# Routing one part of the tokens two slots earlier, and attention's row statistics on ScalarE

## The reference

```python
h = layernorm(patches_of_five_shifted_images @ W.T + b) * gamma + beta      # 36 tokens
h = concatenate([h, vocab[x_txt]], axis=1)                                  # 68 tokens
x = _layernorm(h)
q, k, v = heads(x @ qkv_w.T + qkv_b)                    # 12 heads of 16
_, idx = top_k(_ex_quant(q) @ _ex_quant(k).T, 32)       # exponents only choose the 32 keys
h = h + softmax(true_scores at idx) @ v @ proj_w.T + proj_b
x = _layernorm(h)
w_fk, w_rk = top-4 of softmax((x @ W_fk + b_fk) @ emb_fk_n.T), the same for rk   # of 128 experts each
y = sum over 4 of w_fk * (x @ f_know[e])                # [192] -> [128]
out = h + sum over 4 of w_rk * (y @ r_know[e])          # [128] -> [192]
```

## Time and profile before

| | us |
|---|---|
| median of the runs of before | 963.44 |
| lowest of them | 958.73 |
| the profiled execution, whole | 963.31 |
| its span, first to last instruction | 961.6 |
| mean granted clock of TensorE | 0.841 |
| slots 1 to 32 begin (first and last `sc` addition) | 59.14 to 466.29 |
| first indirect transfer of `send` | 492.86 |
| first product over sorted rows | 550.10 |

### The profile page before, as it was taken

How to read it: one execution, slowest core, us unless ns; L and a number is a source line. 1 busy time by engine, 2 the same in 40 slices (tenths; PEclk the granted TensorE clock), 3 DMA queues, 4 the chain that set the end, 5 groups by cost and what they waited for, 6 DMA issues and landing times.

```text
span 961.6 us, 22280 instructions
## 1 busy us (share of the span) xinstructions
PE 792.3 (82%) x6347; PEld 658.8 (69%) x6347; DVE 657.4 (68%) x4126; ACT 365.6 (38%) x1147; POOL 565.5 (59%) x788
## 2 busy tenths in 40 slices
PE   5789999999999988898664399999998799499800
PEld 4679888888888767776453277999976558355800
DVE  2298999999999979888577367766763364155433
ACT  0133444444444434544323023444431257345700
POOL 5256666767677656575347507506776577775075
PEclk9787989899999868987655579999996899789955
DMA  9332453535353334531047388756799698489533
GB/s 327 107 121 85 182 181 114 183 113 184 114 183 134 114 116 131 173 113 44 13 134 212 121 254 270 221 156 184 243 403 408 224 327 296 147 299 355 194 100 91
DMA packets 81696, 177.25 MB, mean 184 GB/s; under 512 B 12968, under 2 KB 38344, under 8 KB 78760
## 3 DMA queue, kind: packets, MB, share of 16 engines
q1 hardware_dynamic: 56200, 120.62, 37.7%
q10 hardware_dynamic: 14112, 32.12, 8.9%
q0 software_dynamic: 11264, 23.09, 8.0%
HBM read 94.25 MB, written 81.53 MB: 183 GB/s over the span
## 4 chain that ended last, share of the span: by engine, by line
PE 31%; POOL 27%; DVE 16%; issue 14%; DMA 7%; ACT 4%; SPq 1%; POOLq 0%; ACTq 0%; DVEq 0%
POOL early L781 7%; DVE work L1438 6%; PE bank L1301 5%; POOL slots_g L788 5%; DVE top L1432 4%; PE bank L1289 4%; PE bank L1306 3%; POOL slots_x L758 3%; POOL eqbd L653 3%; PE bank L1103 3%; PE bank L1055 2%; PE bank L1035 2%; PE bank L1353 2%; DMA early<-slots_x 2%; POOL sc L704 2%
## 5 line engine op out<-in xcount | busy, mean ns | idle before, releaser
L1438 DVE MATCH_REPLACE8 work<-top,work 128x68 f32<-128x68 f32 x896 | 179.6, 213 | 0.3 <-issue 0.2
L1432 DVE MAX8 top<-work 128x8 f32<-128x68 f32 x896 | 129.3, 215 | 19.7 <-ACT tru L831 19.2
L1740 DVE COPY place<-bank 96x256 f32<-96x256 f32 x147 | 57.1, 416 | 77.2 <-PE bank L1289 73.8
L781 POOL DMA_INDIRECT early<-slots_h,s_all x68 | 65.8, 967 | 57.0 <-DMA slots_h<-m_y 36.9
L758 POOL DMA_INDIRECT slots_x<-early,s_all x68 | 67.8, 998 | 51.1 <-DVE s_all L1622 30.8
L1035 PE MATMUL bank<-early,xp 128*128 128x192 f32 x432 | 92.8, 378 | 5.6 <-DMA xp<-in_a_x 5.2
L781 POOL DMA_INDIRECT early<-slots_y,s_all x68 | 65.2, 959 | 52.2 <-DMA slots_y<-m_y 29.1
L1035 PEld LDWEIGHTS bank<-early,xp 128*128 128x128 f32 x432 | 89.7, 231 | 8.1 <-DMA xp<-in_a_x 5.5
L1748 DVE COPY place<-bank 128x128 f32<-128x128 f32 x147 | 37.6, 287 | 82.3 <-PE bank L1343 80.3
L704 POOL TENSOR_TENSOR sc<-work,tru 128x476 f32<-128x476 f32 x32 | 38.0, 1188 | 78.5 <-ACT work L883 78.5
L788 POOL DMA_INDIRECT slots_g<-early,s_all x68 | 66.4, 976 | 29.9 <-issue 20.1
(11 more groups left out here) (202 smaller groups left out, 1861.7 us busy)
## 6 DMA issues: line engine op xcount, KB each, us to landing
early<-slots_x SPq DMA_DIRECT2D x49, 384.0 KB, 4.1
slots_y<-m_y ACTq DMA_DIRECT2D x49, 384.0 KB
slots_h<-m_y ACTq DMA_DIRECT2D x49, 256.0 KB
early<-slots_g SPq DMA_DIRECT2D x49, 256.0 KB
f_all<-in_f_know SPq DMA_DIRECT2D x16, 768.0 KB, 8.8
r_all<-in_r_know SPq DMA_DIRECT2D x16, 768.0 KB
slots_x<-zero SPq DMA_DIRECT2D x28, 360.0 KB, 3.0
slots_x<-zero SPq DMA_DIRECT2D x28, 336.0 KB, 3.3
```

The source lines that it names most:

```text
L781: nc.gpsimd.indirect_dma_start(g_in[:, i % DEPTH, k, 0:width], None, src, bass.IndirectOffsetOnAxis(s_all[:, r - 1, i, k:k + 1], 0)).then_ ...
L1432: last = nc.vector.max(top8[:, c, :], work[:, par, c, :])
L1438: last = nc.vector.match_replace(work[:, par, c, :], top8[:, c, :], work[:, par, c, :], TAKEN)
L1740: nc.vector.tensor_copy(m_xT[t][0:HALF], turn_bank[t][0:HALF, 0:2 * P].rearrange("p (c s) -> p c s", c=2)).then_inc(sem["m_xt0"], 1)
```

## The change

Part one is routed in slots 22 to 30 (`ROUTE0` is 22). The embedding runs at 8 products a slot throughout and so ends in slot 20, and its last norm is in slot 21. The counting of part one, which stood between slots 32 and 33, is done inside slot 31, and `find_slots` of the first tile inside slot 32. `ahead_of` goes on after part one: tiles 9, 10 and 11 are normalised in slots 30, 31 and 32. GpSimd's slot 33 is gone; its two `finish` steps stand between the first sends.

`norm` leaves VectorE. ScalarE forms the mean by a Copy and the sum of squares by a Square, each with an accumulated output, at the place in the slot where `scale` stood, and `scale` moves behind `copy_scores`. In a routing slot TensorE's `t_query` moves ahead of `attend`, and `t_logits` ahead of `keep_busy` and `t_position`.

The tables and the issuing engine SP:

```diff
-ROUTE0 = 24
+ROUTE0 = 22
...
-    EMBED_AT.setdefault(_n // 8 if _n < 48 else 6 + max(_n - 49, 0) // 7, []).append((2 + _n // CHUNKS_K, _n % CHUNKS_K))
+    EMBED_AT.setdefault(_n // 8, []).append((2 + _n // CHUNKS_K, _n % CHUNKS_K))
...
-            return routed(b + 1)
+            return b + 1 - ROUTE0 if ROUTE0 <= b + 1 <= BATCH + 1 else None
+        NEXT = BATCH + 2 - ROUTE0
...
-                if b in (20, 30, BATCH + 1):
+                if b in (19, 27, 31, BATCH + 1):
...
-                if b == 20:
+                if b == 19:
```

GpSimd:

```diff
-                nc.gpsimd.tensor_tensor(mv[:, 4:5], mv[:, 0:1], minus_one[0:n, :], ALU.mult)
-                nc.gpsimd.tensor_tensor(mv[:, 2:3], mv[:, 1:2], eps_col[0:n, :], ALU.add).then_inc(sem["ln_eps"], 1)
+                nc.gpsimd.tensor_scalar(mv[:, 2:3], mv[:, 1:2], 1.0 / D, EPS, ALU.mult, ALU.add).then_inc(sem["ln_eps"], 1)
...
-                if b == BATCH + 1:
-                    finish(b - 2, par)
...
+            pool.wait_ge(sem["slots_zeroed"], 4 * 16 * N_ZERO)
+            send(0)
+            finish(BATCH - 2, 0)
+            send(1)
+            finish(BATCH - 1, 1)
+            for i in range(NEXT - 4, NT):
...
-            slot(BATCH + 1, 1)
-            pool.wait_ge(sem["slots_zeroed"], 4 * 16 * N_ZERO)
-            for i in range(LED - 1, NT):
-                t_step(i)
-                send(i - LED + 1)
-            for i in range(NT - LED + 1, NT):
+                send(i - NEXT + 6)
```

ScalarE:

```diff
+            def norm(b, par):
+                act.wait_ge(sem[f"hb_in{par}"], own16(b, par))
+                if runs(b, 1, BATCH):
+                    act.wait_ge(sem["ln_done"], b)
+                nc.scalar.activation(xn_flat[:], hb[:, par, :], ACT.Copy, scale=-1.0 / D, accum_out=mv[:, 0:1]).then_inc(sem["ln_stat"], 1)
+                act.wait_ge(sem["ln_stat"], b + 1)
+                nc.scalar.activation(xn_flat[:], hb[:, par, :], ACT.Square, bias=mv[:, 0:1], accum_out=mv[:, 1:2]).then_inc(sem["ln_aggr"], 1)
...
-                    scale(b + 2, par)
+                    norm(b + 2, par)
...
+                if runs(b, 0, BATCH - 3):
+                    scale(b + 2, par)
```

TensorE:

```diff
+                if b == ROUTE0 + LED:
+                    count_part(0)
...
+                if i is not None:
+                    t_query(i)
...
-                if i is not None:
-                    t_query(i)
+                if b == ROUTE0 + LED:
+                    turn_counts(0)
...
-                    if b < BATCH:
-                        keep_busy(i)
+                    t_logits(i)
+                    keep_busy(i)
...
-                    t_logits(i)
...
+                if b == ROUTE0 + LED:
+                    sum_counts(0)
...
-            t_position(LED - 1)
-            count_part(0)
-            turn_counts(0)
-            for i in range(LED - 4, LED - 1):
-                t_step(i)
-            sum_counts(0)
+            t_step(LED - 2)
```

VectorE:

```diff
-            def norm(b, par):
-                dve.wait_ge(sem[f"hb_in{par}"], own16(b, par))
-                nc.vector.bn_stats(stat[:, 0:6], hb[:, par, :]).then_inc(sem["ln_stat"], 1)
-                dve.wait_ge(sem["ln_stat"], b + 1)
-                plain()
-                nc.vector.bn_aggr(mv[:, 0:2], stat[:, 0:6]).then_inc(sem["ln_aggr"], 1)
...
+                counting = b == ROUTE0 + LED
+                if b == BATCH:
+                    find_slots(0, 0)
...
+                if counting:
+                    take_counts(0)
...
-                if runs(b, 0, BATCH - 3):
-                    norm(b + 2, par)
...
+                if counting:
+                    form_counts(0)
...
+                if counting:
+                    form_base(0)
+                    clear_of(0)
...
-            take_counts(0)
-            form_counts(0)
-            form_base(0)
-            clear_of(0)
+            for i in range(1, 4):
+                find_slots(0, i)
```

More of the change, by code:

```diff
@@ L842, in _ @@
             act.wait_ge(sem["biases_in"], 16 * 8)
+            norm(0, 0)
             scale(0, 0)
@@ L846, in _ @@
             copy_scores(0, 0)
+            norm(1, 1)
             scale(1, 1)
@@ L962, in _ @@
             slots_of(act, slot)
-            t_placed(LED - 1)
-            for i in range(LED - 4, LED - 1):
-                t_step(i)
+            t_step(LED - 2)
             slot(BATCH + 1, 1)
@@ L1483, in _ @@
             nc.vector.tensor_tensor(row_b[:, 0, :], bank[1][:, 0:D], row_b[:, 0, :], ALU.add).then_inc(sem["row_ready"], 1)
-            norm(0, 0)
             quantise(0, 0)
-            norm(1, 1)
             def slot(b, m):
@@ L1504, in slot @@
                 i = routed(b)
-                if i is not None and not take:
-                    t_rank(i)
+                if counting:
+                    take_counts(0)
                 if take:
@@ L1528, in slot @@
                     t_aggregate(ahead_of(b))
+                if counting:
+                    form_counts(0)
                 if take:
                     take8(b, par, 2)
-                if i is not None and take:
+                if i is not None:
                     t_rank(i)
+                if counting:
+                    form_base(0)
+                    clear_of(0)
                 if embeds:
@@ L1683, in t_step @@
             def t_step(i):
-                if follows(i + 4):
+                if NEXT <= i + 4 < NT:
                     t_stats(i + 4)
```

31 lines of the change are left out of this document (17 added, 14 removed).

## The result

| | before | after |
|---|---|---|
| median of the runs, us | 961.47 | 1003.46 |
| the profiled execution, whole | 963.31 | 1003.92 |
| its span | 961.6 | 1001.7 |
| mean granted clock | 0.841 | 0.810 |

What follows compares the result with a forecast made beforehand. TensorE and VectorE nearly alike bound slots 6 to 20, TensorE or GpSimd's chain the routing slots, GpSimd the sends; 963.3 + 43.6 (slots 21 to 31) - 20 (tail) - 3 (embedding) = 984 us, range 946 to 998.

Steps and rivals of the forecast that it cites:

- the embedding slots: Slots 6 to 20: 11.9 us each in the mean against 12.08, counted as -3 us for the 15 slots.
- the 0.3 that the low clock costs: Slots 6 to 20: low clock adds 0.3 us to the mean slot of 11.6, giving 11.9.
- The eighth product: TensorE in most of slots 6 to 20: one more embedding product adds 0.33 us at full clock.
- the late `scale`: Slots 6 to 20: `scale` between the copies of the scores and xnT, for which TensorE waits, adds 0.2 to 0.45 us.
- Slots 1 to 5 and the start: Before slot 6: no change counted; slots 1 to 5 had 8 products all along.
- the routing slots: Slots 22 to 29: 19.7 us each, GpSimd's chain waiting behind ScalarE's statistics; slots 21 to 31 together +43.6.
- each slot now has a long stop: Slots 22 to 29: TensorE stops about 2.9 us in every slot, so all run at low clock, 19.7 us each.
- A: The forecast itself: all eight routing slots slow at 19.7, 984 us in all, between 974 and 994; chance 0.42.
- B: Rival: the clock goes on alternating, routing slots 17.3 us in the mean, 965 us in all; chance 0.29.
- The tail: Slot 32 to the first product over sorted rows: -20 us, ends 10 and 22; first send at +6.4, `tile_e` at +64.5.
- D: Rival: routing as forecast, but the tail gives only 10 and `scale` costs embedding slots +5 altogether: 1002 us; chance 0.14.
- The second stage: Everything behind the first product over sorted rows moves along unchanged: 0 us.

Runs made afterwards that it cites:

- E1: The changed kernel with the row statistics back on VectorE and `scale` back in its old place; 953.3 us, ratio 0.990 to the kernel before.
- E13: E1 with only `scale` put behind t_norm and the copies of the scores; 977.5 us, ratio 1.012 to the kernel before.
- E3: The changed kernel with `scale` back in its old place, statistics still on ScalarE behind the copy of oT; 996.7 us, ratio 1.033 to the kernel before.
- E5: E1 with ScalarE's t_norm moved behind the copies of the scores; 952.3 us, ratio 0.992 to the kernel before.
- E7: The changed kernel with ScalarE's statistics early, `scale` in its old place and t_norm behind the scores' copies; 951.0 us, ratio 0.989 to the kernel before.
- E9: The changed kernel with 29 products on zeros ending TensorE's routing slots and 6 more before `queries_keys`; 974.9 us, ratio 1.015 to the kernel before.
- E15: The kernel before with 150 products of ones on TensorE between the product for `tile_e` and the first over sorted rows; 955.1 us, ratio 0.991.
- E4: The changed kernel with ScalarE's statistics moved behind the copy of qk, ahead of the exponentials, `scale` still late; 980.3 us, ratio 1.013 to the kernel before.
- E8: The changed kernel with 20 products on zeros at the end of TensorE's routing slots; 999.4 us, ratio 1.040 to the kernel before.
- E14: E7 with products on zeros in slot 21 (24), ahead of the first t_turn (44) and around it later (4, 8); 938.0 us, 0.971 of before.

## Why the prediction was wrong, by its own steps

**What failed: the embedding slots.** The step was "a plain slot [...] becomes about 11.6", and "the mean of 11.6, with the 0.3 that the low clock costs, is 11.9". The 11.6 was nearly right. At full clock the slots without a norm took 11.33 to 11.66; those with one did not fall to that but to 12.30. One slot in three has a norm, so the mean at full clock is 11.8. The 0.3 was not right: the measured mean of 12.99 makes it 1.2. In the kernel before, the same working gives 11.7 at full clock (12.78 to 12.95 with a norm, 10.95 to 11.19 without one), so 0.4 of the 12.08 was the clock's. The prediction carried this cost over as if it could not grow, and it had itself priced a mean clock of 0.93 at 0.8 a slot in slots 21 and 22.

The most that the clock can cost follows from its two levels. At a mean clock c a share 2(1 - c) of the stretch runs at half speed, and half of that is lost if TensorE bounds it throughout: 0.08 of 12.08, or 0.97 a slot, before, and 0.11 of 12.99, or 1.43, after. Before, 0.4 of the 0.97 showed; after, 1.2 of the 1.43.

The experiments split the step from 12.08 to 12.99. The eighth product cost 0.46 (E1), where 0.33 was written; the late `scale` 0.49 (E13; 0.59 by E3, with the statistics on ScalarE), where 0.2 to 0.45 was. Taking the statistics off VectorE then gave 0.04 (E13 to after), although it gives 0.41 where `scale` keeps its old place (E5 to E7). With the late `scale` the slots with a norm do get shorter at full clock, 12.30 for 12.94, and lower clocks elsewhere take it back: the mean clock is 0.91 to 0.93 in the kernels with `scale` in its old place, and 0.89 or 0.90 wherever `scale` is late with eight products. That VectorE used to hide the low clock, and with more slack no longer does, fits these figures but was not tested by itself. The sum for these slots is off by 16.7 of the 19.9 us by which the forecast of the profiled execution missed.

**Slots 1 to 5 and the start**, counted at nothing, gave +3.9 and +3.4. In slots 1 to 5 it is the late `scale` again: 68.5 in E13 against 62.0 in E1, and over all kernels 67.5 to 68.5 with it against 60.9 to 66.2 without. The start took 61.0 to 62.7 in the ten kernels with the statistics on ScalarE and 59.1 to 61.9 in the seven with VectorE's, so about 1.7 of the 3.4 belongs to the change and the rest to the spread.

**What held: the routing slots.** They were called at 19.7 and are 19.85; slots 21 to 31 were called at +43.6 and gave +44.4. The terms: statistics 1.2, measured 1.03; the chain 3.71, measured 3.63; from t_norm to the copy of xnT 3.30, measured 3.29; TensorE's stop 2.9, measured 2.97. That "each slot now has a long stop" and so none comes at full clock was right, and E9 shows by experiment that it is the stop: filled, the slot is 14.86. For slot 22 the 19.7 came out by another path than the one written, since it began at half clock. Slot 21 (17.61 for 17.6) was right as well; slot 30 (16.94 for 16.4) and slot 31 (13.00 for 14.0) missed in opposite directions. So A's mechanism decided and B's alternating clock did not occur. Of the rule quoted from the Trainium skill's "TensorE: Matmul & The Clock Gate", section "What's actually happening" (activity releases the throttle), E9 and E15 agree: products that compute nothing kept the clock at 1.00.

**The tail**, called at -20, gave -18.2. The first send came 7.69 after slot 32's `sc` addition, not 6.4, and `tile_e` at +63.9. The part of D about the tail was therefore wrong, although its total of 1002 is near the result. Its other part, that `scale` costs every embedding slot, named the right place and priced it at 5 us in all, where slots 1 to 20 gave 17.6 with the eighth product.

**The second stage** was said to move along unchanged and was 7.1 shorter. Its first products ran at half clock for 13.7 us behind the stop of 9.58; after the change the stop was 1.74 and the low clock lasted 3.8. The stage was 5.0 shorter in E15, where TensorE was held busy, and 5.1 shorter in the mean of the kernels whose clock came back early than in that of the others. The other 2 us stay open: within either group the stage varies by 4 to 7.

## What to carry to other kernels

Before moving a step, see which engine in order stands behind it: two activations of 1.03 us cost 3.6 us a routing slot where GpSimd's whole chain hangs behind them (19.85 against 16.21 in E13, with VectorE's statistics and the same late `scale`), and 0.3 where ScalarE was waiting anyway (16.54 in E4). Take (1 - mean clock) times the length of a stretch as the most that the low clock costs in it, expect most of it once TensorE alone is the bound (1.2 of 1.43 a slot here), and ask of each edit whether it gives TensorE one more stop. And what relieving another engine gains hangs on the same stops: taking the statistics off VectorE gained 0.41 a slot with `scale` in its old place (E5 to E7) and 0.04 with it late (E13 to after).

## What the runs showed of the hardware

A stop of TensorE of 3 us costs far more than 3 us: the 12.4 us behind it ran at half clock, and filling it with useless products made the kernel 28.6 us faster. With stops of 0.9 and 0.5 us left in each slot, the clock still fell in most slots (E8). Stops of 0.34 and 0.55 left low stretches that gave a mean clock of 0.87 in slots of 13.65 (E5), and with one stop of 0.9 a slot and products on zeros around it the clock stayed at 1.00 in slots 25 to 29 (E14). So the length of a stop alone doesn't tell whether the clock falls. An activation over 68x192 with an accumulated output takes 0.35 to 0.46 us and 0.19 for the read, which starts before the activation's end in the records; both statistics took 1.03, against 0.34 and 0.18 on VectorE with a wait between them.
